# A new plan of a row's stages, stores by block, and a shorter integer chain, in a one-core kernel of a selective scan over images

## What is computed

```python
xz = layernorm(x) @ W_in;  xh, z = split(xz)            # 512 channels each
xc = depthwise_conv_3x3(xh)                             # over rows and columns
dt_r, B, C = split(xc @ W_xproj)                        # 8, 16, 16
dt = softplus(dt_r @ W_dt + b_dt);  dtN = dt @ W_dtN + b_dtN
for t in range(48 * 48):                                # one state of 512 x 16 per image
    h = exp(dt[t] * A) * h + (dtN[t] * B[t]) * xc[t]
    y[t] = h @ C[t] + Dskip * xc[t]
y = layernorm(y) * ln_g + ln_b
x = x + (y * silu(z)) @ W_out + b_out
v = layernorm(x)
x = x + v + integer_block(v)    # hot bits -> nibbles -> shift left or right -> 2 one-hot additions
```

## Time and profile before

| | us |
|---|---|
| median of 3 runs (lowest to highest) | 4036.85 (4023.55 to 4038.51) |
| profiled execution: its own time | 4022.24 |
| profiled execution: span | 4020.4 |
| first step of the scan begins | 116.35 |
| last step begins | 3981.35 |
| DVE busy | 3622.2 |
| PE busy | 3251.8 |
| POOL busy | 3133.2 |
| ACT busy | 2944.1 |

### The profile page before, as it was taken

The page is one execution under the profiler, slowest core; times in us unless marked ns, Lnnn a source line. Parts: engine busy times, 40 slices in busy tenths (PEclk is TensorE's granted clock), DMA queues, the critical chain, the costliest instruction groups (busy, mean ns, idle before and its releaser), DMA issues.

```text
span 4020.4 us, 103342 instructions
## 1 busy us (share of the span) xinstructions
PE 3251.8 (81%) x33792; PEld 1589.3 (40%) x33792; DVE 3622.2 (90%) x12317; ACT 2944.1 (73%) x6050; POOL 3133.2 (78%) x5771
## 2 busy tenths in 40 slices
PE   5788888888888888888888888888888888888665
PEld 2334433443344334433443344344433343444333
DVE  2799999999999999999999999999999999999996
ACT  3677777777777787777777777777777777787663
POOL 0788877888888788877888788778877888788874
PEclk7889887889889988988898889888888798889776
DMA  3877878788878787878787878787877888788773
GB/s 67 219 202 203 213 191 206 190 208 205 208 196 214 199 211 196 215 194 205 197 216 199 207 196 213 199 205 193 206 201 199 201 203 209 202 206 205 192 192 80
DMA packets 383392, 790.26 MB, mean 197 GB/s; under 512 B 80517, under 2 KB 235142, under 8 KB 382854
## 3 DMA queue, kind: packets, MB, share of 16 engines
q1 hardware_dynamic: 382854, 783.66, 77.1%
HBM read 648.18 MB, written 96.73 MB: 185 GB/s over the span
## 4 chain that ended last, share of the span: by engine, by line
DVE 31%; PE 31%; ACT 26%; issue 7%; SPq 3%; POOL 2%; DMA 1%; ACTq 0%; POOLq 0%; DVEq 0%
ACT ps_a L638 8%; PE ps_s L583 6%; DVE h L885 6%; PE ps_y L492 6%; PE ps_s L528 4%; DVE ps_a L869 4%; DVE ps_a L872 4%; DVE h L888 4%; PE ps_s L537 3%; ACT ap L648 3%; PE ps_s L566 3%; PE ps_y L476 2%; ACT y L721 2%; DVE sz L941 2%; PE ps_s L584 2%
## 5 line engine op out<-in xcount | busy, mean ns | idle before, releaser
L638 ACT ACTIVATE ps_a<-dtb,a_n 128x384 f32<-128x384 f32 x2304 | 1253.6, 583 | 488.1 <-DVE h L888 472.3
L1169 POOL TENSOR_TENSOR h<-mp,up 128x128 f32<-128x128 f32 x2304 | 1052.5, 457 | 357.6 <-PE ps_y L492 147.4
L1159 POOL TENSOR_TENSOR mp<-ap,h 128x128 f32<-128x128 f32 x2304 | 1051.9, 457 | 358.1 <-ACT ap L648 242.7
L869 DVE TENSOR_TENSOR ps_a<-ps_a,h 128x192 f32<-128x192 f32 x2304 | 813.6, 353 | 239.6 <-ACT ps_a L638 236.7
L885 DVE SCALAR_TENSOR_TENSOR h<-xb,db,ps_a 128x192 f32<-128x192 f32 x2304 | 921.9, 400 | 24.0 <-PE ps_y L492 16.0
L888 DVE SCALAR_TENSOR_TENSOR h<-xb,db,ps_a 128x192 f32<-128x192 f32 x2304 | 927.2, 402 | 0.0
L492 PE MATMUL ps_y<-h,cw 64*32 64x256 f32 x18432 | 787.9, 461 | 71.9 <-DVE h L888 58.0
L872 DVE TENSOR_TENSOR ps_a<-ps_a,h 128x192 f32<-128x192 f32 x2304 | 807.7, 351 | 0.0
L648 ACT ACTIVATE ap<-dtb,a_n 128x256 f32<-128x256 f32 x1152 | 524.2, 509 | 251.1 <-DMA dtb<-xd 233.9
L1149 POOL TENSOR_TENSOR up<-xb,db 128x512 f32<-128x512 f32 x576 | 610.8, 1060 | 3.0 <-DMA xb<-xd 3.0
L492 PEld LDWEIGHTS ps_y<-h,cw 64*32 64x32 f32 x18432 | 315.7, 122 | 488.2 <-DVE h L888 244.6
(11 more groups left out here) (111 smaller groups left out, 4286.5 us busy)
## 6 DMA issues: line engine op xcount, KB each, us to landing
xb<-xd SPq DMA_DIRECT2D x576, 512.0 KB, 7.2
dtb<-xd SPq DMA_DIRECT2D x576, 512.0 KB, 6.3
xs<-xh SPq DMA_DIRECT2D x196, 192.0 KB, 6.2
xd<-dttok SPq DMA_DIRECT2D x288, 128.0 KB, 5.4
xin<-in_x_dram SPq DMA_DIRECT2D x144, 128.0 KB, 6.2
xd<-xtok SPq DMA_DIRECT2D x192, 96.0 KB
res<-in_x_dram SPq DMA_DIRECT2D x144, 128.0 KB, 5.4
out_dram<-res SPq DMA_DIRECT2D x144, 128.0 KB, 3.9
```

The source lines that it names most:

```text
L638: ins = act.activation(ps_a[buf][:, n, 0:2 * VD].rearrange("p (t d) -> p t d", t=2), dtb[:, u % DUNITS, 2 * buf:2 * buf + 2, 0:VD], ACT.Ex ...
L869: dve.tensor_tensor(a[:, 0], a[:, 0], last[:, 0], ALU.mult).then_inc(m0_done, 1)
L1159: pool.tensor_tensor(mp[:, G % 2], ap[:, Q % 2, G % 4], h[:, (G - 1) % HRING, :, VD:HALF], ALU.mult) \
L1169: pool.tensor_tensor(h[:, G % HRING, :, VD:HALF], mp[:, G % 2], up[:, Q % 2, G % 4], ALU.add) \
```

## The change

It sets new slots for every stage, moves the convolution one row further ahead (`AHEAD` 2) and the projection one row less (3), stores `xtok` and `dttok` in three parts each, moves SP's other transfers, and rewrites the integer block as 12 stages instead of 14, one to a slot, in slots 0 to 11 of the next row instead of slots 40 to 46. The sizes of the matrix products, the transfers and the scan's own instructions stay as they are. The core of the diff:

```diff
 SLOT = {
-    "conv": (0, 1, 3, 4), "xproj": (6,), "dtp": (8, 9, 11, 12), "xtok": (14, 15, 16), "yt": (18, 19, 20, 21),
-    "dttok": (23, 24, 26), "dtn": (27,), "out": (29, 30, 31), "z": (33, 34, 36, 37), "xlnT": (39, 40),
-    "proj": (42, 43, 45, 46),
+    "proj": (0, 2, 10, 11), "xproj": (1,), "dtp": (3, 4, 21, 22), "xtok": (6, 7, 9), "yt": (16, 17, 18, 19),
+    "out": (23, 24, 25), "z": (27, 28, 29, 30), "dtn": (31,), "dttok": (32, 33, 35), "conv": (40, 41, 42, 43),
+    "xlnT": (45, 46),
 }
...
-                    if s == 6 and exists(i - 2):
+                    if s in (8, 10, 12) and exists(i + 1):
+                        store_x(i + 1, (8, 10, 12).index(s))
+                    if s == 13 and 0 <= i + 3 <= SIDE:
+                        load_stack(i + 3)
+                    if s == 14 and exists(i - 2):
                         store(i - 2)
...
-                    if s == 18 and exists(i - 1):
+                    if s == 19 and exists(i - 1):
                         load_residual(i - 1)
...
-                    if s == 30 and exists(i + 1):
+                    if s == 34 and exists(i + 1):
                         bounce_states(i + 1)
-                    if s == 34 and exists(i + 1):
+                    if s in (35, 36, 38) and exists(i + 1):
+                        store_dt(i + 1, (35, 36, 38).index(s))
+                    if s == 37 and exists(i + 1):
                         load_states(i + 1)
...
-                        if s == 11:
+                        if s == 9:
                             softplus_exp(i + 1, 0)
-                        if s == 14:
+                        if s == 12:
+                            softplus_log(i + 1, 0)
+                        if s == 24:
                             softplus_exp(i + 1, 1)
-                        if s == 15:
-                            softplus_log(i + 1, 0)
-                        if s == 16:
+                        if s == 25:
                             softplus_log(i + 1, 1)
...
-                        if s in (14, 15, 16):
-                            y_norm(i - 1, s - 14)
+                        if s in (13, 14, 15):
+                            y_norm(i - 1, s - 13)
...
-                    ins = dve.tensor_scalar(hot[:], hot[:], 0.5, None, ALU.is_gt)
+                    for w in range(3):
+                        ins = dve.scalar_tensor_tensor(score[:, :, w, :], hot[:, :, 32 + 8 * w:48 + 8 * w], 0.5,
+                                                       score16[:].unsqueeze(1).broadcast_to([P, KT, 16]),
+                                                       ALU.is_gt, ALU.mult)
...
-                elif n == 4:
-                    ins = dve.tensor_scalar(found[:], best[:], 0.0, None, ALU.is_gt)
-                elif n == 5:
-                    ins = dve.tensor_scalar(best[:], best[:], -1.0, 16.0, ALU.mult, ALU.add)
-                elif n == 6:
-                    ins = dve.tensor_tensor(nib[:], best[:], found[:], ALU.mult)
...
-                    if s in (30, 31, 32):
-                        add_residual(i - 1, s - 30)
-                    if s in (33, 34, 35):
-                        ln2_stats(i - 1, s - 33)
...
+                    if s in (24, 25, 26):
+                        add_residual(i - 1, s - 24)
+                    if s in (26, 27, 28):
+                        ln2_stats(i - 1, s - 26)
...
-                    if s in (34, 35, 37, 38):
-                        make_sz(i, (34, 35, 37, 38).index(s))
+                    if s in (29, 30, 31, 32):
+                        make_sz(i, s - 29)
...
-                    if s in (16, 17) and exists(i + 1):
-                        finish_dt(i + 1, s - 16)
+                    if s in (13, 26) and exists(i + 1):
+                        finish_dt(i + 1, (13, 26).index(s))
...
-                    if s in (21, 22, 23, 24) and exists(i - 1):
-                        gate_y(i - 1, s - 21)
+                    if s in (18, 19, 20, 21) and exists(i - 1):
+                        gate_y(i - 1, s - 18)
```

More of the change, by code:

```diff
@@ L148, in build @@
         best = sb("best", [P, KT, 3])
-        found = sb("found", [P, KT, 3])
         nib = sb("nib", [P, KT, 3], I32)
@@ L344, in load_stack, with store_x @@
                       .then_inc(xs_loaded, SEM_DMA)
-            def store_x(r):
-                sp.wait_ge(xtok_ready, r * KT + KT)
-                if r >= 2:
+            def store_x(r, block):
+                sp.wait_ge(xtok_ready, r * KT + block + 1)
+                if r >= 2 and block == 0:
                     for n in range(XUNITS):
                         sp.wait_ge(x_loaded[n], (r - 1) * (QUADS // XUNITS) * SEM_DMA)
-                for k, lo, n, j, q0 in X_PARTS:
+                for k, lo, n, j, q0 in X_PARTS[2 * block:2 * block + 2]:
                     for half in range(2):
@@ L355, in store_x, with store_dt @@
                           .then_inc(x_stored, SEM_DMA)
-            def store_dt(r):
-                sp.wait_ge(dttok_ready, r * KT + KT)
-                if r >= 2:
+            def store_dt(r, k):
+                sp.wait_ge(dttok_ready, r * KT + k + 1)
+                if r >= 2 and k == 0:
                     for n in range(DUNITS):
                         sp.wait_ge(dt_loaded[n], (r - 1) * (QUADS // DUNITS) * SEM_DMA)
-                for k in range(KT):
-                    for half in range(2):
-                        sp.dma_start(xd[r % 2, 1, half, :, 16 * k:16 * k + 16, :].rearrange("b w d -> w b d"),
-                                     dttok[:, k * DI + half * HALF:k * DI + (half + 1) * HALF]) \
-                          .then_inc(dt_stored, SEM_DMA)
+                for half in range(2):
+                    sp.dma_start(xd[r % 2, 1, half, :, 16 * k:16 * k + 16, :].rearrange("b w d -> w b d"),
+                                 dttok[:, k * DI + half * HALF:k * DI + (half + 1) * HALF]) \
+                      .then_inc(dt_stored, SEM_DMA)
             def spread(which, r, k):
@@ L983, in ffn_stage @@
                     ins = dve.tensor_tensor(amp[:], hot[:, :, 39], hot[:, :, 40], ALU.max)
                 elif n == 3:
-                    dve.scalar_tensor_tensor(amp[:], amp[:], 2.0, hot[:, :, 0], ALU.mult, ALU.mult)
-                    ins = dve.tensor_reduce(best[:], score[:], AX_X, ALU.max)
+                    dve.tensor_scalar(nib[:], best[:], -1.0, 16.0, ALU.mult, ALU.add)
+                    ins = dve.tensor_scalar(amp[:], amp[:], 0.5, 2.0, ALU.is_gt, ALU.mult)
                 elif n == 4:
-                    ins = dve.tensor_scalar(found[:], best[:], 0.0, None, ALU.is_gt)
+                    dve.tensor_single_scalar(nib[:], nib[:], 15, ALU.bitwise_and)
@@ L989, in ffn_stage @@
+                    ins = dve.scalar_tensor_tensor(amp[:], hot[:, :, 0], 0.5, amp[:], ALU.is_gt, ALU.mult)
                 elif n == 5:
[L990 removed]
+                    ins = dve.scalar_tensor_tensor(val[:], nib[:, :, 1], 16.0, nib[:, :, 0], ALU.mult, ALU.add)
                 elif n == 6:
[L992 to L995 removed]
@@ L1134, in _ @@
                     after(i, s)
+            for n in range(FFN):
+                ffn_stage(SIDE - 1, n)
+            ffn_mark(SIDE - 1)
+            ffn_weigh(SIDE - 1)
             ffn_add_low(SIDE - 1)
```

135 lines of the change are left out of this document (58 added, 77 removed).

## The result

The changed kernel takes 4393.6 us (median of 4 runs, 4392.1 to 4395.1), the one before 4030.2 (4 runs beside it): ratio 1.090, 95% interval 1.087 to 1.093. The forecast was 4225 with a range up to 4380: the direction is right, but the loss is 363 us against the runs beside it where 197 was forecast, and the time lies outside the range.

The account below looks back on a forecast made before the run. DVE was taken to bound the kernel; new waits of 11.6 us a row, less 5.5 of old waits and 2.0 of DVE work, gave +4.1 a row, +197 over 48 rows, hence 4225 us, range 3920 to 4380.

Parts of the forecast that it names:

- DVE sets the pace: Whole row: DVE's own work is 75.1 of 80.6 us, and other engines only cost what they make it wait.
- Where the new waits are: DVE waits at step 24 (2.6 us), 25 and 26 (2.4), 32 (2.1), 44 (2.5), and for ACT (2.0): 11.6 a row.
- POOL's way to the gates: POOL's work from its state of step 12 through four gates: 17.7 us, ending 22.0 us after DVE's step 8.
- Rival 1: POOL runs earlier, so the first two new waits, 5.0 us a row, vanish: 3979 or 3883 us; chance 0.24.
- Integer block, −2.0: DVE's rewritten integer block: removed and merged instructions save 2.0 us a row, bounds 0.8 and 2.8.
- The sum: Per row: new waits 11.6 less old waits 5.5 less DVE work 2.0 gives +4.1 us, +197 over 48 rows.
- Rival 2: PE at 1.2 GHz after waiting for the gates: one `out` block adds 1.8 us a row, 4311 us; chance 0.11.
- Rival 3: Row's start: first `dtb` waits for `dttok` stores behind `load_states` and bounce, at most 3.1 us a row, 4368 us; chance 0.08.
- Old waits, −5.5: DVE's existing waits for decays, output product and PE's sums, 5.5 us a row, all go.

Follow-up runs that it names:

- finish_later: The changed kernel with POOL's sum of the first half of softplus moved from slot 13 to slot 16: 4396.1 us, ratio 1.094 to the kernel before.

## Why the prediction was right and wrong

The step that failed is "DVE sets the pace", and with it the sum: it adds what DVE's own work saves to what DVE waits, and leaves PE's low clock out. By the terms, the waits are 1.3 us a row too small and DVE's work 2.8 too small (−2.0 forecast, +0.8 measured). DVE's busy time, forecast to fall by some 100 us, rose by 28.5. By the runs, the row is closed by a loop through POOL, PE and ACT, in which DVE's work of steps 4 to 24 has no part and PE works at the low clock in three places.

- *Where the new waits are*: right. Forecast 2.6 at step 24, 2.4 at 25 and 26, 2.1 at 32, 2.5 at 44 and 2.0 for ACT, 11.6; measured in slots 23 and 24 3.0, in 25 and 26 2.1, in 31 and 32 2.4, in 40 to 44 5.3, with little ones 12.9. That the waits of step 24 and of the convolution come from these places was shown by moving them (3.9 and 1.7 us a row).
- *POOL's way to the gates*: right to 0.1 us in its end, partly by luck in its beginning. In row 20 it ends 21.95 us after DVE's step 8 (1897.77 to 1919.72), forecast 22.0. But POOL was held at step 8, where it waited 2.71 us for the sum behind the slow skip product, and not at step 12; from there it had no other wait for PE, and the sum of slot 12, which I took as the bound, was done 0.3 us before POOL wanted it. Rival 1 is refuted.
- *Integer block, −2.0*: wrong. It became 10.1 us from 8.2. I counted the instructions that go and not the two that come, `nib & 15` and the comparison for `amp`, which take 0.92 and 0.41 us here. And most of the time of the removed ones was POOL's: 8.2 to 7.8 when only the code changes. One stage a slot beside POOL's `up`, together with the sum in slot 13, costs more collisions, the merged comparison alone 0.9. My bounds were savings of 0.8 to 2.8; the lower one should have reached into a loss, since the earlier trace rows already showed what a small instruction meets.
- *Not costed at all*: the shifts of the two norms, 1.7 us a row with POOL in front of them, 0.2 now. Without this DVE's work would be 1.5 us higher still: the block's step is 3.9 us off, the work as a whole 2.8.
- *The sum*: wrong in form. I added DVE's work and waits as if DVE were on the path in every slot. 0.7 us less of DVE's work in slots 12 and 13 gave nothing (`finish_later`), and the old block, 1.9 us a row shorter, gives the same row. So the block's 96 us of forecast gain were not to be had on this plan by this much less work, and a right size for the block would not have mended the forecast.
- *Rival 2, the clock*: came true beside the forecast, not instead of it, as the earlier trace rows had it: 3.77 us. I held it as an alternative with 0.11; it belonged in the sum. It is in the loop at slot 23 and, not foreseen, at 40 (8.80 + 1.93 + 1.96 where I took 1.02, 1.09 and blocks of the earlier trace rows, 10.3 in all) and at slot 8. Filling the wait at 40 alone gave 1.9 us a row. How the 4.0 us a row that were missed divide between the clock and the rest of the loop, no run shows.
- *Rival 3, the next row's first `dtb`*: refuted; no wait at the row's start, and the bounce lands in 1.7 us in the changed kernel, where the earlier trace rows had 7.1.
- *Old waits, −5.5*: right, and they go by the block's place as much as by the plan: on the old plan with the new block in its new place 2.5 of them go.

## What to carry to other kernels

When a row of work repeats, follow the chain of the changed order once round before adding up gains: only what lies on the loop counts, and a gain on an engine off the loop comes back as its idle time at the next joint. Price PE's work on the loop at the clock that it has behind a wait. An instruction whose mean is long because it stands behind another engine gives little back when it is removed (0.4 us a row here), since the next one may stand there instead; work of an engine that is ahead belongs where another engine is late. Keep distance in slots between a producer chain (POOL's gates) and the product that everything queues behind, and let a sum that others wait for go ahead of the block that only one consumer needs.

## What the runs showed of the hardware

- A single tensor comparison of 128x96 took 1261 ns in the mean with a POOL sum of 1.8 us in its slot and 339 ns with that sum three slots later; in the last row of the second kernel, where POOL is done, it took 259.
- Filling a wait with products at 1.2 GHz is dear: 10 instructions took 4.63 us there, 16 at the higher clock 3.72.
